# Attention kernel: the row sums' PSUM bank becomes a fourth work bank, and ScalarE copies the sums to SBUF

## The chip, the cores and the metric

The kernel runs on one core of one Trainium2 chip. The metric is the device time of one execution in microseconds. The kernel before took 1515.11 us, the median of three runs (1514.18 to 1516.34).

## What is computed

Two attention layers over a batch of 8 images of 256 channels and 1024 positions, in fp32. Layer 0 has a group normalisation and 8 heads of 32 channels; layer 1 has one head whose queries and keys have 32 channels and whose values have 256. Cut to what matters:

```python
# layer 0, B = 8, C = 256, T = 1024, 8 heads of ch = 32
h = groupnorm(x, 32 groups) * gn_w + gn_b
q, k, v = qkv_w @ h + qkv_b
w = softmax((q * ch**-0.25)^T (k * ch**-0.25))      # T x T for each head
x = x + proj_w @ (v w^T) + proj_b
# layer 1
energy = (Wq x)^T (Wk x)                             # T x T
x = x + gamma * (Wv x) softmax(energy)^T
```

## The kernel before

**Tiling.** An image's layer 0 is worked in two groups of four heads (g) and two chunks of 512 queries (c): four chunks, ci = 2g + c. A chunk goes over 8 blocks of 128 keys; for a block and a pair of heads there is one slot, in which TensorE makes two score products of 128 keys by 512 queries into PSUM (`st`, three banks used in turn), ScalarE takes the exponential of each into `probs` (a ring of nine slots in SBUF, line 789), and GpSimd adds the slots up into `acc` (lines 901 to 906 and 925). Every eight slots TensorE multiplies the exponentials with the values into the bank `pv` (line 574), in a group of 32 instructions. Layer 1 of the image before has eight slots of its own, 48 to 55, with products at line 596. So an image has 72 slots, and each slot has three stops.

**Maxima.** The softmax subtracts each query's maximum. It is found ahead of time: TensorE makes the same scores with queries on the partitions (lines 651 and 659), and VectorE reduces each bank (lines 954 and 957). That is 128 products per image in layer 0 and 16 in layer 1. The maxima are transposed (lines 664 and 667), split in two parts (lines 970 and 972) and put under the queries as two more rows by DMA.

**Work banks.** The maxima, their transposes, queries and keys (QK, line 714), values (VT, line 721; VT1, line 685), the projection (P, line 673) and the small products of the normalisation use a cycle of three PSUM banks, `work`. `fill_bank` (line 631) takes the next bank in turn, and TensorE waits there until the bank's last user, three entries before, has been read (`wait_used`). VectorE or ScalarE reads it; QK is read by both. ScalarE's own uses are counted apart (`SCALAR_USES`, line 156).

**Sums and quotients.** When a chunk's exponentials are added up in `acc`, a product with ones (`fill_rec`, line 605) sums them over the partitions into a bank of its own, `rec` (line 243). VectorE makes the reciprocals in place in PSUM in four pieces of 128 columns (line 1042; two pieces in layer 1, line 1054). After the last piece it multiplies `attn`, which ScalarE has copied from `pv`, with `rec` (line 1047). In layer 1 it multiplies each half of the raw output by gamma and `rec`, into `rec` (line 1060, twice), and adds `y` into `xa` (line 1063). Before a new sum TensorE waits for the last quotient (`wait_rec_free`, line 312). So these steps have one input in PSUM and one in SBUF. In the normalisation, lines 998 and 999 compute the same difference into PSUM and into SBUF, and line 1001 multiplies the two.

**Order.** Every engine has its own stream, in order. TensorE, ScalarE and VectorE go through the same plan (`plan_of`, line 106): tables by kind of image (`FIRST`, `STEADY`, `LAST`, `EPILOGUE`, lines 45 to 97) give for each entry of a chain the stop at which it stands, with 216 stops in an image. In the chain of sums an entry SUM is followed by its four reciprocals, in that of layer 1 by two. TensorE makes the sums of a slot at its end (line 735). ScalarE serves its entries behind the slot's exponentials, ahead of them in some slots (line 849). SP's queue issues the DMAs that stack queries and keys (24 for each group, `stack_rows`, line 390) and the transfers of inputs, maxima and output; GpSimd issues none.

```python
ST_BANKS, WORK_BANKS = 3, 3                                            # line 32
if i >= WORK_BANKS:                                                    # line 634
    wait_used(pe, banks[kind][i - WORK_BANKS], kind, b)
for e in ready:                                                        # line 735
    fill_rec(e, kind, b)
```

Of the kernel before, what the change touches and what calls it, by code (L numbers as in the profile page):

```python
# [5 lines left out]
F32 = mybir.dt.float32  # L6
# [25 lines left out]
ST_BANKS, WORK_BANKS = 3, 3  # L32
# [7 lines left out]
def places(*counts):  # L40
# [5 lines left out]
    "maxima1": (56, 60, 71, 73, 74, 76, 82, 99, 100, 101, 103, 103, 107, 108, 113, 114, 122, 125),  # L46
    "qk1": (193, 196, 196, 203),
    "norm": (27, 34, 35, 42, 52, 70, 84, 100, 109, 110, 120),
# [3 lines left out]
    "layer1": (4, 7, 32, 33, 38, 55, 88, 112, 139),  # L52
    "v1": (14, 16),
    "maxima": places(1, 0, 1, 2, 2, 2, 1, 0, 0, 1, 2, 2, 0, 0, 0, 3, 1, 1, 1, 1, 0, 0, 1, 0, 2, 0, 1, 0, 0, 0, 1,
# [6 lines left out]
}  # L61
FIRST = {
    "qf": (7, 7, 8, 8),
    "maxima0": (12, 12, 16, 21, 22, 22, 24, 24, 24, 24, 24, 26, 26, 28, 28, 28),
    "qk1": (158, 193, 208, 208),
    "norm": (29, 29, 29, 42, 48, 64, 64, 107, 108, 110, 112),
    "sums": (63, 72, 95, 97, 108, 112, 122, 151, 155, 157, 162, 166, 185, 203, 206),
    "v0": (193, 211),
    "v1": (32, 50),
    "maxima": places(4, 1, 0, 1, 1, 0, 0, 0, 0, 0, 0, 0, 0, 0, 0, 4, 0, 1, 0, 0, 0, 1, 0, 0, 2, 0, 0, 1, 0, 0, 1,  # L70
# [6 lines left out]
}  # L77
LAST = {
    "maxima1": (58, 60, 62, 63, 66, 73, 81, 82, 83, 88, 91, 94, 95, 95, 110, 112, 125, 125),
    "sums": (9, 11, 26, 30, 32, 56, 57, 67, 111, 122, 143, 152, 155, 155, 156, 163, 165, 166, 167, 167),  # L80
    "sums1": (159, 160, 163, 169, 170, 170, 171, 174, 174, 174, 175, 175),
    "layer1": (14, 24, 38, 39, 41, 67, 70, 106, 113),
    "v1": (32, 119),
    "maxima": places(0, 0, 2, 0, 2, 0, 0, 1, 0, 0, 3, 1, 1, 0, 1, 0, 0, 1, 0, 1, 2, 0, 2, 0, 0, 0, 0, 0, 3, 0, 1,
# [6 lines left out]
}  # L91
EPILOGUE = {
    "sums": (3, 3, 6, 6, 10),
# [12 lines left out]
def plan_of(kind):  # L106
# [1035 lines left out]
```

## Time and profile before

| | us |
|---|---|
| median of three runs | 1515.11 |
| lowest, highest run | 1514.18, 1516.34 |
| span of the profiled execution | 1513.1 |
| TensorE busy (matmuls) | 1476.9 |
| TensorE weight loads | 892.7 |
| GpSimd busy | 1168.3 |
| VectorE busy | 1099.3 |
| ScalarE busy | 745.2 |

The profiled execution's span goes from its first to its last instruction; no time of its own with what lies around it is given, so it is set beside the runs. Matmuls are pipelined and each is drawn longer than the distance to the next, so a busy TensorE is not one at its peak; how often weight loads wait, and for whom, says more. The other engines' busy times add up as they are. Line numbers such as L954 are those of the kernel. PE is TensorE, PEld its weight loads, DVE VectorE, ACT ScalarE, POOL GpSimd.

### The profile page before, as it was taken

What the parts mean: (1) busy time and instruction counts of PE and PEld (TensorE: products, weight loads), DVE (VectorE), ACT (ScalarE), POOL (GpSimd) and SP (SyncE); (2) the same over time, 40 slices, a digit from 0 to 9 for tenths busy, and PEclk for the clock granted to TensorE, in tenths of its full rate; (3) what the DMA queues carried; (4) which work ended last, traced back from release to release, by engine and by line L of the source; (5) the groups of instructions that cost most, each with busy time, mean ns of one, the idle gap of its engine ahead of it and who ended that gap; (6) DMA issues with size and microseconds to landing.
All of it is one profiled execution on the core that took longest, in us unless ns stands there. A gap on an engine that the chain in (4) does not pass through costs nothing.

```text
span 1513.1 us, 20608 instructions
## 1 busy us (share of the span) xinstructions
PE 1476.9 (98%) x7248; PEld 892.7 (59%) x7248; DVE 1099.3 (73%) x1922; ACT 745.2 (49%) x1373; POOL 1168.3 (77%) x540
## 2 busy tenths in 40 slices
PE   8899999999999999999999999999999999999988
PEld 6454455567555765558555675557655585556547
DVE  4777868787787878877687777878778776775343
ACT  2356446644566355653556445563546536554412
POOL 2278579985899678994899858997789949898704
PEclk8799999999999999999999999999999999999979
DMA  5223132120503014030421205030140303100100
GB/s 150 48 67 78 36 74 60 38 48 31 139 22 85 15 48 113 17 85 22 106 64 30 56 22 147 23 84 15 44 112 22 85 21 98 44 1 8 49 21 29
DMA packets 47143, 85.24 MB, mean 56 GB/s; under 512 B 11072, under 2 KB 21184, under 8 KB 47040
## 3 DMA queue, kind: packets, MB, share of 16 engines
q1 hardware_dynamic: 46896, 83.74, 22.0%
q8 instruction: 57, 0.93, 0.3%
q14 instruction: 46, 0.38, 0.1%
q10 hardware_dynamic: 144, 0.20, 0.1%
HBM read 18.29 MB, written 8.39 MB: 18 GB/s over the span
## 4 chain that ended last, share of the span: by engine, by line
PE 82%; DVE 8%; ACT 4%; SPq 2%; issue 2%; DMA 1%; POOL 0%; ACTq 0%; DVEq 0%; POOLq 0%
PE pv L596 15%; PE pv L574 15%; PE st L565 14%; PE work L651 13%; PE work L714 7%; DVE mpart L954 6%; PE work L673 3%; PE work L721 3%; PE work L685 3%; ACT probs L789 2%; PE st L557 2%; SPq L396 2%; PE rec L615 2%; PE work L659 2%; PE work L679 1%
## 5 line engine op out<-in xcount | busy, mean ns | idle before, releaser
L925 POOL TENSOR_TENSOR acc<-acc,probs 128x1024 f32<-128x1024 f32 x372 | 871.0, 2380 | 19.8 <-ACT probs L789 18.9
L789 ACT ACTIVATE probs<-st 128x512 f32<-128x512 f32 x1152 | 610.6, 602 | 422.1 <-PE st L565 201.2
L954 DVE TENSOR_REDUCE mpart<-work 128x1 f32<-128x512 f32 x1008 | 636.1, 678 | 136.3 <-PE work L651 133.8
L651 PE MATMUL work<-ks,qs 96*128 96x512 f32 x1008 | 430.5, 469 | 9.2 <-DMA ks<-part_hi 2.4
L565 PE MATMUL st<-qs,ks 98*128 98x512 f32 x1024 | 395.7, 429 | 7.0 <-DMA qs<-mrow 3.1
L925 POOL TENSOR_TENSOR acc<-probs 128x1024 f32<-128x1024 f32 x64 | 151.1, 2373 | 191.4 <-ACT probs L789 191.3
L651 PEld LDWEIGHTS work<-ks,qs 96*128 96x128 f32 x1008 | 190.6, 193 | 143.2 <-DVE mpart L954 68.0
L565 PEld LDWEIGHTS st<-qs,ks 98*128 98x128 f32 x1024 | 193.3, 191 | 119.1 <-ACT probs L789 65.3
L596 PE MATMUL pv<-probs,l_vt 128*128 128x256 f32 x1024 | 240.8, 381 | 0.7 <-ACT xa L862 0.5
L574 PE MATMUL pv<-probs,vt 128*32 128x512 f32 x2048 | 236.3, 602 | 0.0
L596 PEld LDWEIGHTS pv<-probs,l_vt 128*128 128x128 f32 x1024 | 193.8, 191 | 35.8 <-ACT probs L789 5.9
L901 POOL TENSOR_TENSOR acc<-probs 128x1024 f32<-128x1024 f32 x32 | 75.4, 2356 | 116.6 <-ACT probs L789 108.3
L574 PEld LDWEIGHTS pv<-probs,vt 128*32 128x32 f32 x2048 | 60.6, 111 | 139.6 <-issue 137.9
L1042 DVE RECIPROCAL rec<-rec 128x128 f32<-128x128 f32 x128 | 117.4, 941 | 7.4 <-PE rec L615 4.1
L714 PE MATMUL work<-h,wqkv 128*128 128x512 f32 x256 | 119.3, 600 | 2.0 <-ACT h L842 1.9
L984 DVE SCALAR_TENSOR_TENSOR part_lo<-work,qkbs,part_hi 128x512 fp32r<-128x512 f32 x60 | 44.4, 749 | 76.9 <-ACT part_hi L813 76.9
L957 DVE TENSOR_REDUCE mpart_l<-work 128x1 f32<-128x512 f32 x128 | 83.1, 679 | 20.7 <-PE work L659 20.4
L1054 DVE RECIPROCAL rec<-rec 128x128 f32<-128x128 f32 x64 | 57.5, 936 | 45.7 <-PE rec L628 45.7
L714 PEld LDWEIGHTS work<-h,wqkv 128*128 128x128 f32 x256 | 47.3, 191 | 47.7 <-issue 39.0
L813 ACT ACTIVATE part_hi<-work,qkbs 128x512 fp32r<-128x512 f32 x60 | 41.2, 687 | 65.3 <-PE work L714 65.3
L862 ACT COPY xa<-pv 128x512 f32<-128x512 f32 x32 | 18.8, 587 | 108.1 <-PE pv L596 108.1
L721 PEld LDWEIGHTS work<-wqkv,h 128*128 128x128 f32 x512 | 61.5, 192 | 4.1 <-ACT vt L818 1.4
(82 smaller groups left out, 953.4 us busy)
## 6 DMA issues: line engine op xcount, KB each, us to landing
qs<-part_hi SPq DMA_DIRECT2D x120, 128.0 KB, 2.4
ks<-part_hi SPq DMA_DIRECT2D x120, 128.0 KB, 2.4
xa<-in_x SPq DMA_DIRECT2D x16, 512.0 KB, 4.4
y<-in_x SPq DMA_DIRECT2D x8, 1024.0 KB, 6.1
out<-xa SPq DMA_DIRECT2D x32, 256.0 KB, 2.2
qs<-part_lo SPq DMA_DIRECT2D x60, 128.0 KB, 2.4
ks<-part_lo SPq DMA_DIRECT2D x60, 128.0 KB, 2.4
l_qs<-part_hi SPq DMA_DIRECT2D x32, 64.0 KB, 2.0
```

Source lines behind the costliest of these rows:

```text
L565: mm(bank, ks[g][0:ROWS, j, blk * P:(blk + 1) * P], qs[g][0:ROWS, c, j, :], start=True, stop=True).then_inc(s_st0, 1)
L574: last = mm(pv[CH * j:CH * (j + 1), :], vt[:, blk, g * P + CH * j:g * P + CH * (j + 1)], probs[:, (n - 1 + j // 2) % PRING, (j % 2) * HALF ...
L596: last = mm(pv[:, m * QUARTER:(m + 1) * QUARTER], vt1[:, 4 * (i % 2) + q, m * P:(m + 1) * P], probs[:, n % PRING, q * QUARTER:(q + 1) * QU ...
L651: last = mm(bank, qs[g][0:HI_HI_LO, c, j, tb * P:(tb + 1) * P], ks[g][0:HI_HI_LO, j, half * HALF:(half + 1) * HALF], start=True, stop=True)
L714: last = mm(bank, wqkv[:, k, col:col + P], h[:, k, n * HALF:(n + 1) * HALF], start=(k == 0), stop=(k == KT - 1))
L721: last = mm(bank[:, s * P:(s + 1) * P], h[:, k, blk * P:(blk + 1) * P], wqkv[:, k, 2 * C + g * P:2 * C + (g + 1) * P], start=(k == 0), sto ...
L789: nc.scalar.activation(probs[:, n % PRING, half * HALF:(half + 1) * HALF], st[:, (2 * n + half) % ST_BANKS, :], ACT.Exp).then_inc(s_exp1 i ...
L901: pool.tensor_tensor(a, probs[:, (n - 1) % PRING, :], probs[:, n % PRING, :], ALU.add).then_inc(s_add1, 1)
L925: pool.tensor_tensor(a, first, probs[:, n % PRING, :], ALU.add).then_inc(s_add0, 1)
L954: last = dve.reduce_max(mpart[:, 4 * j + tb, half:half + 1], bank, AX.X)
L957: last = dve.reduce_max(mpart1[:, tb, half:half + 1], bank, AX.X)
L1042: dve.reciprocal(r, r).then_inc(s_rec, 1)
```

## The change

The bank `rec` in PSUM is gone; `work` has four banks, and `rec` is a tensor of 512 columns in SBUF. The sums SUM and SUM1 are entries of the cycle of work banks now: `sum_rows` makes the same products into the next work bank, at the entry's own stop instead of the end of its slot. ScalarE copies the bank to `rec` (512 columns, or 256 in layer 1), and before it waits that the last quotient has been made; TensorE doesn't wait for that any more. VectorE's reciprocals and quotient steps are the same instructions, with `rec` in SBUF. VectorE waits for ScalarE's copy, GpSimd and the exponentials of the last part for the fill of the bank, instead of for the sums' own counter. At one point of the first image VectorE waits for its own reduction of the last early maximum (M0). The tables of stops are new throughout; the lines of sums in the steady images, and those of the second group's queries and keys (QF) in the first, are shown.

```diff
-ST_BANKS, WORK_BANKS = 3, 3
+ST_BANKS, WORK_BANKS = 3, 4
 STEADY = {
-    "sums": (10, 14, 14, 16, 23, 72, 74, 75, 100, 118, 134, 135, 135, 141, 146, 153, 154, 154, 154, 157),
-    "sums1": (159, 159, 159, 162, 164, 164, 170, 171, 175, 175, 193, 193),
+    "sums": (10, 14, 14, 16, 23, 72, 74, 75, 100, 119, 134, 135, 137, 141, 147, 154, 159, 159, 159, 159),
+    "sums1": (159, 162, 162, 162, 166, 166, 168, 168, 168, 171, 189, 193),
...
 FIRST = {
-    "qf": (7, 7, 8, 8),
+    "qf": (3, 3, 3, 5),
...
-NO_BANK = ("SUM", "SUM1", "MC", "MC1", "BN", "AGG", "H", "R", "R1")
-SCALAR_USES = ("VT", "VT1")
+NO_BANK = ("MC", "MC1", "BN", "AGG", "H", "R", "R1")
+SCALAR_USES = ("VT", "VT1", "SUM", "SUM1")
...
+        rec = sb("rec", [P, HALF])
...
-        rec = ctx.enter_context(nc.psum_tensor("rec", [P, HALF], F32))
...
-            eng.wait_ge(s_sum, sum_no(e, kind, b) + 1)
+            eng.wait_ge(s_w, w_base(kind, b) + place[kind][e] + 1)
...
-            def fill_rec(e, kind, b):
-
-                wait_rec_free(pe, e, kind, b)
-                if e[0] == "SUM":
...
+            def sum_rows(e, bank, kind, b):
+
+                if e[0] == "SUM1":
+                    pe.wait_ge(s_add1, ADDS1 * (b - 1) + 3 * (e[1] + 1))
+                    return mm(bank[:, 0:QUARTER], ones[:, :], acc1[e[1] % 2][:, 0:QUARTER], start=True, stop=True)
+                _, g, c = e
...
+                pe.wait_ge(s_add0, adds_until(bb, ci + 1) - (2 * LEFT if kind == "epilogue" else 0))
+                for j in range(GH):
+                    last = mm(bank[CH * j:CH * (j + 1), :], ones[:, 0:CH],
+                              acc[:, c, j // 2, (j % 2) * HALF:(j % 2 + 1) * HALF], start=True,
+                              stop=not left, tile_position=(0, CH * j))
...
+                elif what in ("SUM", "SUM1"):
+                    last = sum_rows(e, bank, kind, b)
...
-                    for e in ready:
-                        fill_rec(e, kind, b)
...
+                elif e[0] in ("SUM", "SUM1"):
+                    wait_rec_free(act, e, kind, b)
                 act.wait_ge(s_w, w_base(kind, b) + i + 1)
...
+                elif e[0] == "SUM":
+                    last = nc.scalar.copy(rec[:, :], bank)
+                elif e[0] == "SUM1":
+                    last = nc.scalar.copy(rec[:, 0:QUARTER], bank[:, 0:QUARTER])
...
                     if p == 0:
-                        wait_summed(dve, ("SUM", g, c), kind, b)
+                        wait_used(dve, ("SUM", g, c), kind, b)
...
                     if p == 0:
-                        wait_summed(dve, ("SUM1", c), kind, b)
+                        wait_used(dve, ("SUM1", c), kind, b)
...
+                    if kind == "first" and (g, c) == (0, 1):
+                        wait_used(dve, ("M0", 1, 3, 1), kind, b)
                     wait_used(dve, ("M", g, c, GH - 1, 3, 1), kind, b)
```

## Rows read from the trace of the kernel before

**Rows 1.** the head of the page: span, busy time of each engine

```profile
span 1513.1 us, 20608 instructions
...
PE 1476.9 (98%) x7248; PEld 892.7 (59%) x7248; DVE 1099.3 (73%) x1922; ACT 745.2 (49%) x1373; POOL 1168.3 (77%) x540
```

**Rows 2.** table by windows: the first image and a later one (us from the start)

```profile
core 0: us, PE busy (x) PEld busy (x) DVE busy (x) ACT busy (x) POOL busy (x), PEclk, DMA share, GB/s
58.00:240.00 182.00, 176.84 (x823) 87.28 (x823) 136.22 (x242) 92.97 (x171) 129.13 (x56) 0.97 0.29 71
417.00:594.00 177.00, 175.53 (x891) 108.40 (x890) 137.44 (x241) 92.71 (x171) 148.73 (x69) 1.00 0.24 59
```

**Rows 3.** timeline of TensorE: start us, us, instruction

```profile
487.51 0.39 PE L565 MATMUL st<-qs,ks 98*128 98x512 f32 x1
487.74 0.39 PE L651 MATMUL work<-ks,qs 96*128 96x512 f32 x1
```

**Rows 4.** table of waits, whole run: us in total, times, longest us

```profile
PEld work L651 <- DVE mpart L954: 68.0, 207, 0.8
PEld st L565 <- ACT probs L789: 65.3, 230, 0.8
...
PEld work L659 <- DVE mpart L954: 12.6, 20, 0.8
...
PEld work L651 <- DVE mpart_l L957: 9.2, 31, 0.6
```

**Rows 5.** table of waits, first image alone (58 to 240 us)

```profile
PEld work L651 <- DVE mpart L954: 21.7, 57, 0.8
```

**Rows 6.** groups of instructions: busy us, mean ns of one, idle before

```profile
L954 DVE TENSOR_REDUCE mpart<-work 128x1 f32<-128x512 f32 x1008 | 636.1, 678 | 136.3 <-PE work L651 133.8 <-issue 0.2
L789 ACT ACTIVATE probs<-st 128x512 f32<-128x512 f32 x1152 | 610.6, 602 | 422.1 <-PE st L565 201.2 <-PE pv L574 96.6 <-PE st L557 96.6
...
L651 PEld LDWEIGHTS work<-ks,qs 96*128 96x128 f32 x1008 | 190.6, 193 | 143.2 <-DVE mpart L954 68.0 <-issue 31.4 <-DVE mpart_l L957 9.2
...
L1042 DVE RECIPROCAL rec<-rec 128x128 f32<-128x128 f32 x128 | 117.4, 941 | 7.4 <-PE rec L615 4.1 <-PE rec L622 3.2
...
L1047 DVE TENSOR_TENSOR attn<-attn,rec 128x512 f32<-128x512 f32 x32 | 22.0, 687 | 1.8 <-ACT attn L872 0.7
L1070 DVE BATCH_NORM_STATS2 bst<-xa 128x6 f32<-128x512 f32 x32 | 20.2, 679 | 9.1 <-DMA xa<-in_x 9.1
...
L872 ACT COPY attn<-pv 128x512 f32<-128x512 f32 x32 | 18.8, 587 | 60.3 <-PE pv L574 60.3
```

**Rows 7.** timeline of GpSimd, 417 to 594 us

```profile
472.56 28.06 POOL L925 TENSOR_TENSOR acc<-acc,probs 128x1024 f32<-128x1024 f32 x12
...
515.35 2.35 POOL L901 TENSOR_TENSOR acc<-probs 128x1024 f32<-128x1024 f32 x1 [5.72 <-ACT probs L789]
517.77 1.28 POOL L904 TENSOR_TENSOR acc<-acc 128x512 f32<-128x512 f32 x1
519.14 0.73 POOL L906 TENSOR_TENSOR acc<-acc 128x256 f32<-128x256 f32 x1
...
543.94 28.02 POOL L925 TENSOR_TENSOR acc<-acc,probs 128x1024 f32<-128x1024 f32 x12
```

**Rows 8.** timeline of VectorE, same stretch: quotient steps

```profile
476.84 0.69 DVE L1047 TENSOR_TENSOR attn<-attn,rec 128x512 f32<-128x512 f32 x1
...
516.59 1.01 DVE L1060 SCALAR_TENSOR_TENSOR rec<-xa,gam,rec 128x256 f32<-128x256 f32 x2
...
551.27 1.01 DVE L1060 SCALAR_TENSOR_TENSOR rec<-xa,gam,rec 128x256 f32<-128x256 f32 x2
```

**Rows 9.** the chain in order of time: start us, us, what

```profile
514.74 3.45 PE pv L596 x16
519.57 3.45 PE pv L596 x16
...
551.82 3.57 PE pv L574 x32
```

More of the change, by code:

```diff
@@ L45 @@
 STEADY = {
-    "maxima1": (56, 60, 71, 73, 74, 76, 82, 99, 100, 101, 103, 103, 107, 108, 113, 114, 122, 125),
-    "qk1": (193, 196, 196, 203),
-    "norm": (27, 34, 35, 42, 52, 70, 84, 100, 109, 110, 120),
-    "sums": (10, 14, 14, 16, 23, 72, 74, 75, 100, 118, 134, 135, 135, 141, 146, 153, 154, 154, 154, 157),
-    "sums1": (159, 159, 159, 162, 164, 164, 170, 171, 175, 175, 193, 193),
-    "v0": (181, 206),
-    "layer1": (4, 7, 32, 33, 38, 55, 88, 112, 139),
-    "v1": (14, 16),
-    "maxima": places(1, 0, 1, 2, 2, 2, 1, 0, 0, 1, 2, 2, 0, 0, 0, 3, 1, 1, 1, 1, 0, 0, 1, 0, 2, 0, 1, 0, 0, 0, 1,
[6 rows of a table removed]
+    "maxima1": (56, 60, 69, 74, 74, 76, 82, 96, 104, 104, 104, 104, 107, 108, 113, 114, 116, 123),
@@ L61 @@
+    "qk1": (189, 192, 195, 203),
+    "norm": (25, 26, 27, 42, 52, 69, 84, 98, 106, 110, 120),
+    "sums": (10, 14, 14, 16, 23, 72, 74, 75, 100, 119, 134, 135, 137, 141, 147, 154, 159, 159, 159, 159),
+    "sums1": (159, 162, 162, 162, 166, 166, 168, 168, 168, 171, 189, 193),
+    "v0": (181, 206),
+    "layer1": (4, 7, 29, 33, 38, 55, 89, 112, 138),
+    "v1": (12, 16),
+    "maxima": places(2, 0, 0, 2, 2, 3, 1, 0, 0, 2, 2, 0, 0, 0, 0, 3, 1, 1, 1, 1, 0, 0, 0, 1, 2, 0, 1, 0, 0, 0, 0, 2, 1,
[6 rows of a table added]
 }
@@ L62 @@
 FIRST = {
-    "qf": (7, 7, 8, 8),
[L64 to L70, printed above, removed]
[6 rows of a table removed]
+    "qf": (3, 3, 3, 5),
+    "maxima0": (8, 8, 8, 8, 8, 10, 14, 14, 14, 15, 22, 23, 25, 26, 27, 27),
@@ L77 @@
+    "qk1": (159, 190, 205, 210),
+    "norm": (29, 29, 29, 42, 48, 59, 62, 105, 105, 107, 109),
+    "sums": (67, 72, 96, 98, 103, 113, 123, 149, 156, 158, 163, 164, 186, 205, 208),
+    "v0": (190, 212),
+    "v1": (31, 48),
+    "maxima": places(4, 1, 0, 1, 1, 0, 0, 0, 0, 0, 0, 2, 0, 0, 0, 2, 0, 1, 0, 0, 0, 1, 0, 0, 0, 3, 0, 0, 1, 0, 0, 0, 0,
[6 rows of a table added]
 }
 LAST = {
-    "maxima1": (58, 60, 62, 63, 66, 73, 81, 82, 83, 88, 91, 94, 95, 95, 110, 112, 125, 125),
-    "sums": (9, 11, 26, 30, 32, 56, 57, 67, 111, 122, 143, 152, 155, 155, 156, 163, 165, 166, 167, 167),
@@ L81 @@
[L81 to L84, printed above, removed]
[6 rows of a table removed]
+    "maxima1": (58, 60, 62, 62, 62, 76, 77, 82, 83, 88, 93, 94, 95, 95, 109, 111, 121, 126),
+    "sums": (9, 11, 26, 30, 32, 56, 57, 67, 110, 121, 144, 145, 151, 154, 155, 162, 165, 165, 168, 169),
+    "sums1": (159, 160, 161, 169, 170, 170, 171, 174, 174, 174, 175, 178),
@@ L91 @@
+    "layer1": (4, 22, 34, 37, 43, 67, 71, 107, 113),
+    "v1": (12, 105),
+    "maxima": places(0, 0, 2, 0, 2, 0, 0, 1, 0, 0, 2, 0, 0, 0, 4, 1, 0, 1, 0, 2, 2, 0, 0, 0, 0, 0, 4, 0, 0, 0, 0, 0, 0,
[5 rows of a table added]
 }
 EPILOGUE = {
-    "sums": (3, 3, 6, 6, 10),
[3 rows of a table removed]
+    "sums": (2, 2, 2, 2, 2),
[3 rows of a table added]
 }
@@ L603, in product_l1 @@
                         fill_bank(e, kind, b)
-            def fill_rec(e, kind, b):
-                wait_rec_free(pe, e, kind, b)
-                if e[0] == "SUM":
-                    _, g, c = e
-                    ci = 2 * g + c
-                    bb = b - 1 if ci == 3 else b
-                    left = LEFT if kind == "epilogue" else 1 if bb == 0 else 0
-                    pe.wait_ge(s_add0, adds_until(bb, ci + 1) - (2 * LEFT if kind == "epilogue" else 0))
-                    for j in range(GH):
-                        last = mm(rec[CH * j:CH * (j + 1), :], ones[:, 0:CH],
-                                  acc[:, c, j // 2, (j % 2) * HALF:(j % 2 + 1) * HALF], start=True,
-                                  stop=not left, tile_position=(0, CH * j))
-                    if left:
-                        wait_exp(pe, last_slot(ci), bb)
-                    for blk in range(left):
-                        for j in range(GH):
-                            last = mm(rec[CH * j:CH * (j + 1), :], ones[:, 0:CH],
-                                      probs[:, (last_slot(ci) - 2 * left + 1 + 2 * blk + j // 2) % PRING,
-                                            (j % 2) * HALF:(j % 2 + 1) * HALF],
-                                      start=False, stop=blk == left - 1, tile_position=(0, CH * j))
-                else:
-                    pe.wait_ge(s_add1, ADDS1 * (b - 1) + 3 * (e[1] + 1))
-                    last = mm(rec[:, 0:QUARTER], ones[:, :], acc1[e[1] % 2][:, 0:QUARTER], start=True, stop=True)
-                last.then_inc(s_sum, 1)
@@ new lines, in sum_rows @@
+            def sum_rows(e, bank, kind, b):
[3 more added lines that the diff above has]
+                _, g, c = e
+                ci = 2 * g + c
+                bb = b - 1 if ci == 3 else b
+                left = LEFT if kind == "epilogue" else 1 if bb == 0 else 0
+                pe.wait_ge(s_add0, adds_until(bb, ci + 1) - (2 * LEFT if kind == "epilogue" else 0))
[3 more added lines that the diff above has]
+                              stop=not left, tile_position=(0, CH * j))
+                if left:
+                    wait_exp(pe, last_slot(ci), bb)
+                for blk in range(left):
+                    for j in range(GH):
+                        last = mm(bank[CH * j:CH * (j + 1), :], ones[:, 0:CH],
+                                  probs[:, (last_slot(ci) - 2 * left + 1 + 2 * blk + j // 2) % PRING,
+                                        (j % 2) * HALF:(j % 2 + 1) * HALF],
+                                  start=False, stop=blk == left - 1, tile_position=(0, CH * j))
+                return last
@@ L728, in step @@
                     stops = [[e for e in plans[kind][STOPS * n + k] if e[0] not in NO_BANK] for k in range(STOPS)]
-                    ready = [e for k in range(STOPS) for e in plans[kind][STOPS * n + k] if e[0] in ("SUM", "SUM1")]
                     for half in range(2):
@@ L915, in step @@
                         if ci == 0 and kind != "first":
-                            pool.wait_ge(s_sum, sum_no(sums[kind][0], kind, b))
+                            wait_summed(pool, ("SUM", 1, 0), "first" if b == 1 else "steady", b - 1)
                         elif ci == 1 and kind != "first":
@@ L1090, in step @@
                     for e in entries:
-                        if e[0] in ("H", "SUM", "SUM1"):
+                        if e[0] == "H":
                             continue
```

1 line of the change is left out of this document (removed), and 41 rows, old and new, of tables (EPILOGUE, FIRST, LAST, STEADY).

## The prediction

> **What bounds the kernel now.** I read the page's head first. TensorE is busy for all but 36 us of 1513.1, VectorE for 73% [rows 1]. A busy TensorE is not one at its peak, so next come two stretches of the table by windows: the first image, 182 us, and a later one, 177 us; here all engines but TensorE have room on average, GpSimd least (148.7 of 177) [rows 2]. How fast TensorE can go is seen where nothing is late, in its timeline: score and maxima products of 512 columns start some 0.23 us apart (487.51, 487.74), though each is drawn 0.39 us long [rows 3]. What holds it beyond that is in the table of waits, in the rows of the weight loads: 68.0 us in 207 waits for VectorE's maxima over work banks, 12.6 and 9.2 us more of the same sort, and 65.3 us in 230 waits for ScalarE's exponentials over score banks [rows 4]. A load has about 0.05 us between it and the next anyway (0.24 less the 0.19 that it takes [rows 6]), so these waits are stalls less 0.05 us each. Work banks: 89.8 us in 258 waits, less 13, is 77 us, some 5% of the time. That is the ceiling for a fourth work bank. Of it, 21.7 us in 57 waits, 19 after the same deduction, lie in the first image [rows 5]; some 58 us are spread over the rest.
>
> **The change, part by part.** The sum is made against the profiled span of 1513.1 us; the runs shown lie 1.1 to 3.2 us above it, their median 2.0.
>
> *A fourth work bank, tables anew.* A maximum holds its bank for VectorE's 678 ns [rows 6], while TensorE makes a product in 0.24. Every further bank lets a burst run on for one more reduction, which takes 0.68 − 0.24 = 0.44 us off the waits of that burst. Outside the first image the waits average 0.33 us and come in twos and threes, so one bank should remove most: I take two thirds of 58, 38 us. In the first image bursts are long, and there VectorE's rate decides: 8 of 19. Gain 46 us. Bounds: none (the stalls turn into other waits) and 77. The new tables move entries by a few stops, with what they issue: the second group's queries and keys of the first image go from stops 7 to 8 to stops 3 to 5, and the 24 stacking transfers on SP's queue behind them start earlier; nothing is queued there that is due before. I cost this at nothing beyond the bank's gain.
>
> *64 sums in the cycle of banks.* The same products, with the same changes of tile, so no TensorE time. TensorE no longer waits for the quotient before a sum, but for a work bank. It waited little for quotients before, so nothing is won.
>
> *64 copies on ScalarE.* 32 of 512 columns at 587 ns [rows 6], 18.8 us; 32 of 256 columns, between 0.29 (half) and 0.587 us, I take 0.37, 11.8 us. ScalarE is busy 92.7 of 177 us [rows 2], so most of these 31 us are covered by its idle time. But a copy can stand in front of an exponential for which TensorE waits. It waits for 230 of 1152 [rows 4, 6], a fifth, and not each of those has a copy before it: I take a tenth, 3 us; bounds 0 and 31.
>
> *The wait for the last quotient moves to ScalarE.* Exponentials are queued behind it, and TensorE, GpSimd and the score banks wait for these. The sum of group 1, chunk 0 has its four reciprocals all at stop 159, beside the first layer-1 sum, whose copy waits for that quotient: four times 0.94 us and 0.69 us [rows 6] is 4.5 us of VectorE in front of it. Three score banks and the lag of two slots between scores and products give TensorE about one layer-1 slot, 4.8 us (product groups start 514.74 and 519.57 on the chain [rows 9]), so I take 0; the bound above is 2 us in each of 7 images, 14.
>
> *192 reciprocals in SBUF.* In PSUM 128 columns take 941 ns. 512 columns out of SBUF (batch statistics, 679 ns) and out of PSUM (maxima, 678 ns) cost VectorE the same [rows 6]; I take 0, between the 0.1 us each (19 us of VectorE time) that I could not exclude either way. The Trainium skill, page "VectorE: DVE Perf Modes", section on the TRN2 errata, gives a fixed 58 cycles for sources in SBUF and 120 for PSUM; by it the reciprocals would win 65 ns each, 12 us of VectorE time in all, which the two equal rows speak against.
>
> *128 quotient steps with two inputs in SBUF.* These are the 32 of line 1047, 64 of line 1060, 32 of line 1063. Until now each has one input in PSUM, and so has every other large VectorE operation here with two tensors; lines 998 and 999 even make the same difference twice, into PSUM and into SBUF, so that the product of the two has one of each. What a second SBUF input costs beside GpSimd, which reads SBUF all the time, no row shows. Lower bound 0: VectorE takes 0.49 or 0.69 us as now. Upper bound: each waits for the end of GpSimd's addition in progress, and GpSimd's next one slips in between two of them. Laid over one image: additions run back to back from 472.56, 2.34 us each; a chain 515.35 to 517.70, then 1.28, then 0.73; again without a break from 543.94 [rows 7]. Of an image's eight quotients three find GpSimd idle. Of the layer-1 ones, that at 516.59 would wait 1.1 + 1.3 + 0.7 = 3.1 us, that at 551.27 2.0 + 2.3 + 2.3 = 6.6; three of layer 0, as at 476.84 with its 0.4 [rows 8], 0.9 together. That is 10.6 us in an image, 74 in seven. At 516.59 the products of layer 1 fill 3.45 of the 4.8 us of a slot [rows 9] and leave work banks free. That at 551.27 meets a full stretch, but 3.57 us of it lie under the product group from 551.82, which needs no work bank [rows 9]. So 6.6 − 3.6 = 3.0 us reach TensorE in each image. I take this upper case for VectorE: 21 us over seven images. Bounds 0 and 74.
>
> *The small rest.* Line 1083 of VectorE waits once for a reduction of its own queue, long done. Waits on the fill counters replace those on the sums' counter at the same moments. GpSimd would be held for the quotient steps themselves, 1.7 us at the last one of an image, ahead of its own idle time. All at nothing; cover: GpSimd's 28 us of idle time in an image [rows 2].
>
> Sum: −46 + 3 + 0 + 0 + 21 = −22. 1513.1 − 22 = 1491, with 2 around the span **1493 us**.
>
> **Rivals.**
> *Slower: the quotient steps wait, and what is queued behind them waits too.* Place: the end of each quotient, from line 1047 on. Price: the whole 10.6 us an image, 74 us, if the stretches around them are dense, plus 14 for ScalarE's stand behind the quotient, less 46 won: +42, some 1557; with half of the 74, plus 14 and 3, it is +8, 1523. It decides from the point where more than 46 − 3 = 43 us of waits reach TensorE, 6 us an image. For it: VectorE goes from 137.4 to 148 of 177 us, and reciprocals, reductions and quotients share one queue; the last steps hold query and key banks, too. Against it: half of the layer-1 quotients meet no addition, and the rest lie beside products. The Trainium skill states the mechanism ("SBUF — State Buffer", section "SBUF: two separate sides"): VectorE with two SBUF inputs and a GpSimd operation that reads SBUF exclude each other for a whole instruction. By that rule the quotient waits worked out above are real, and only their reach is open. Middle of this case: 1535. Chance 0.32.
> *Faster than forecast: the second SBUF input costs nothing.* Then −46 + 3 = −43, or 1472; with the ceiling of the bank 1450 at most. For it: no row shows any contention. Chance 0.17.
> *No change: the stalls move.* Waits for score banks are nearly as many (65.3 us in 230 [rows 4]), and a TensorE that is held less by work banks may only reach those sooner; or gain and price cancel. 1512 to 1518. Chance 0.12.
> *Forecast.* The bank's gain is seen, the quotients cost some of it: 1480 to 1510. Chance 0.39.
>
> **Numbers.** Likeliest 1493. Below, the range takes in the case without contention (1470); above, it goes into the slower case to 1540. About 0.2% is what a measurement of this kernel can tell from no change. Faster 0.39 + 0.17 = 0.56; same 0.12; slower 0.32.
>
> **What would show it.** Weight loads' waits for work banks should fall from 90 to some 45 us. The quotient steps should start late after their reciprocals, or be drawn longer than 0.49 and 0.69 us, where GpSimd is in an addition, and GpSimd's additions beside them longer than 2.4 us: were all still 0.49 and 0.69 without gaps, the contention is refuted. ScalarE should be busy some 31 us more. Waits for exponentials much over 65 us, with ScalarE waiting for the quotient, would show its queue as the new bound. If VectorE's waits stay and the time still rises, the forecast is wrong by the reach of the quotient steps.

## The result and the profile after

The changed kernel takes 1674.97 us (median of four runs, 1672.45 to 1681.12), against 1514.71 us for the kernel before on the same chip: a ratio of 1.1067, 95% interval [1.1042, 1.1092]. It was forecast at 1493 us, in a range from 1470 to 1540. The profiled execution spans 1670.6 us, 157.5 more than before. Every ratio in this document is that of fast runs alone; a run more than 1.5% above the fastest one of its kernel counts as slow, and two runs below do.

The head of the page of the kernel after, and TensorE's granted clock in 40 slices:

```profile
span 1670.6 us, 20737 instructions
...
PE 1501.0 (90%) x7248; PEld 928.4 (56%) x7248; DVE 1296.0 (78%) x1922; ACT 772.5 (46%) x1437; POOL 1175.6 (70%) x540
...
PEclk8799989898998989989899899989999899899989
```

Beside [rows 1], TensorE is idle for 169.6 us instead of 36.2, and VectorE is busy 196.7 us more. The mean granted clock of the profiled execution went from 0.978 to 0.932. With the two levels of 2.4 and 1.2 GHz (1 and 0.5) that is 0.044 and 0.136 of the span at the lower one, an estimate of 67 and 227 us.

The groups of instructions of the kernel after (busy us, mean ns of one | idle before); the lines are some numbers further down than in [rows 6]:

```profile
L926 POOL TENSOR_TENSOR acc<-acc,probs 128x1024 f32<-128x1024 f32 x372 | 871.6, 2378 | 119.2 <-ACT probs L784 118.8
L955 DVE TENSOR_REDUCE mpart<-work 128x1 f32<-128x512 f32 x1008 | 632.2, 678 | 126.6 <-PE work L647 125.0
...
L1048 DVE TENSOR_TENSOR attn<-attn,rec 128x512 f32<-128x512 f32 x32 | 157.3, 4916 | 1.1
...
L1043 DVE RECIPROCAL rec<-rec 128x128 f32<-128x128 f32 x128 | 115.1, 926 | 20.5 <-ACT rec L827 20.5
L1061 DVE SCALAR_TENSOR_TENSOR rec<-xa,gam,rec 128x256 f32<-128x256 f32 x64 | 93.7, 1465 | 5.7 <-ACT xa L863 3.5
...
L1064 DVE TENSOR_TENSOR xa<-rec,y 128x512 f32<-128x512 f32 x32 | 27.0, 845 | 1.1
...
L827 ACT COPY rec<-work 128x512 f32<-128x512 f32 x32 | 18.7, 585 | 18.5 <-PE work L614 10.2 <-PE work L621 7.2 <-DVE xa L1064 0.2
...
L829 ACT COPY rec<-work 128x256 f32<-128x256 f32 x32 | 11.9, 373 | 38.2 <-PE work L607 23.3 <-DVE xa L1064 9.9 <-PE work L647 4.1
```

Everything but the quotient steps has its old duration, the reciprocals out of SBUF too (926 ns after 941). The 32 products of line 1048 took 4916 ns each, after 687 [rows 6]; those of line 1061 took 1465 after 490, those of 1064 took 845 after 691. In sum VectorE stood in these three lines for 135.3 + 62.4 + 4.9 = 203 us longer. How the 203 us are spread matters: 23 of the 128 steps were drawn over 3.2 us long, 17 of line 1048 and 6 of line 1061, and they hold 182 us of it. GpSimd's additions still take 2.38 us on average: it hardly waited for VectorE. ScalarE's copies cost 18.7 + 11.9 us, as forecast.

The table of waits of the kernel after (us in total, times, longest us):

```profile
ACT probs L784 <- PE st L563: 346.1, 171, 26.4
...
PEld work L647 <- DVE part_lo L985: 93.7, 14, 8.3
...
PE work L647 <- DVE part_lo L985: 87.2, 13, 7.9
...
PEld work L647 <- DVE mpart L955: 55.4, 132, 1.5
```

Waits of the weight loads for maxima fell from 68.0 us in 207 times [rows 4] to 55.4 in 132. That is no clean measure of the fourth bank, since TensorE stood still elsewhere; the run with one-input steps below gives one. In their place stand fourteen waits, up to 8.3 us long, for a bank of queries or keys (part_lo), whose reader on VectorE, in the place shown next, is queued behind a quotient step; the two rows for them tell of the same waits, once at the weight load and once at the product. ScalarE, for its part, waits 346 us for scores, after 201.2 [rows 6].

One such place, first on GpSimd's timeline of the kernel after (start us, us, instruction):

```profile
504.11 16.26 POOL L926 TENSOR_TENSOR acc<-acc,probs 128x1024 f32<-128x1024 f32 x7
```

on VectorE's:

```profile
507.26 0.94 DVE L1043 RECIPROCAL rec<-rec 128x128 f32<-128x128 f32 x1
508.23 12.69 DVE L1048 TENSOR_TENSOR attn<-attn,rec 128x512 f32<-128x512 f32 x1
520.85 0.74 DVE L985 SCALAR_TENSOR_TENSOR part_lo<-work,qkbs,part_hi 128x512 fp32r<-128x512 f32 x1
```

on ScalarE's:

```profile
523.58 0.60 ACT L784 ACTIVATE probs<-st 128x512 f32<-128x512 f32 x1 [8.77 <-PE st L563]
```

on TensorE's:

```profile
513.10 0.73 PE L563 MATMUL st<-qs,ks 98*128 98x512 f32 x2
521.64 1.39 PE L647 MATMUL work<-ks,qs 96*128 96x512 f32 x2 [7.80 <-DVE part_lo L985]
...
524.97 0.63 PE L647 MATMUL work<-ks,qs 96*128 96x512 f32 x1
525.39 0.63 PE L563 MATMUL st<-qs,ks 98*128 98x512 f32 x1
...
528.43 0.39 PE L647 MATMUL work<-ks,qs 96*128 96x512 f32 x1
528.66 0.40 PE L563 MATMUL st<-qs,ks 98*128 98x512 f32 x1
```

and in the table by windows over the same stretch:

```profile
core 0: us, PE busy (x) PEld busy (x) DVE busy (x) ACT busy (x) POOL busy (x), PEclk, DMA share, GB/s
...
516.00:520.00 4.00, 0.00 (x0) 0.00 (x0) 4.00 (x1) 0.00 (x0) 4.00 (x2) 0.71 0.00 0
520.00:524.00 4.00, 2.36 (x5) 1.72 (x6) 3.97 (x8) 0.42 (x1) 0.38 (x1) 0.50 0.29 66
524.00:528.00 4.00, 4.00 (x14) 1.40 (x14) 2.32 (x4) 1.88 (x4) 2.55 (x2) 0.51 0.61 135
528.00:532.00 4.00, 4.00 (x18) 3.19 (x18) 3.29 (x5) 2.77 (x6) 4.00 (x2) 1.00 0.88 197
```

The product of line 1048 starts at 508.23 and ends at 520.92. All that time GpSimd goes through seven additions without a gap (504.11 to 520.37), and 0.55 us after the last the product is done. So it didn't wait only for the addition in progress, which ended at 508.8; it waited for that one and the five behind it. The reader of the keys' bank follows at 520.85, and TensorE, which had come to that bank at 513.8, starts again at 521.64. GpSimd's run ended because of that: TensorE's standstill stopped the scores, and ScalarE had waited 8.77 us for them when it made its next exponential at 523.58. The granted clock falls while TensorE stands (0.71 in the window from 516, no product in it) and is 0.50 and 0.51 in the windows to 528, its lower level: two products of 512 columns are 0.42 us apart there (524.97, 525.39), and 0.23 us again at 528.43 and 528.66, at the upper one. Of the 128 quotient steps 17 were drawn over 8 us long, and with all 17 the granted clock falls to 0.50, during the step or within 0.2 us of its end.

**Not every addition goes first.** Another step of line 1048, on GpSimd's timeline and on VectorE's:

```profile
841.63 2.39 POOL L926 TENSOR_TENSOR acc<-acc,probs 128x1024 f32<-128x1024 f32 x1 [0.33 <-ACT probs L784]
843.99 2.82 POOL L926 TENSOR_TENSOR acc<-acc,probs 128x1024 f32<-128x1024 f32 x1
```

```profile
843.00 1.57 DVE L1048 TENSOR_TENSOR attn<-attn,rec 128x512 f32<-128x512 f32 x1
```

These two additions follow each other without idle time, too. Yet the product got in between them: it was done 0.55 us after the first, and the second was drawn 2.82 us instead of 2.38. The timelines of the whole run have 77 ends of an addition at which a quotient step was waiting and the next addition followed without idle time. At 69 of them the addition went first, at 8 the step. Count the additions of an unbroken run from the one that starts after idle time, be it 0.08 us. Then all 69 are ends of the third or a later addition of an unbroken run; four of the 8 are ends of a first and two of a second, and the other two are a third and a fourth right behind steps that had been let in. The runs below say the same: no end of a first or second addition was passed over in any, and none of a fifth or later one let a step in. So it takes an unbroken run of some length, three to five additions here, before VectorE is starved. Why that is so no run shows.

### The profile page after: what moved, and what is told of

It reads as the page before. It is cut to its first block, busy times and chain, and to the rows that moved or that the text cites. A ratio compares the mean times of both kernels' runs of the same rounds, so it can differ in the third digit from the quotient of the medians.

```text
span 1670.6 us, 20737 instructions
## 1 busy us (share of the span) xinstructions
PE 1501.0 (90%) x7248; PEld 928.4 (56%) x7248; DVE 1296.0 (78%) x1922; ACT 772.5 (46%) x1437; POOL 1175.6 (70%) x540
## 4 chain that ended last, share of the span: by engine, by line
PE 67%; DVE 19%; issue 7%; SPq 4%; ACT 2%; DMA 1%; ACTq 0%; DVEq 0%; POOL 0%; POOLq 0%
PE pv L594 13%; PE st L563 12%; PE work L647 11%; PE pv L572 8%; DVE mpart L955 6%; PE work L712 6%; DVE rec L1061 4%; PE work L669 4%; DVE attn L1048 3%; PE work L681 3%; SPq L394 2%; PE work L614 2%; DVE rec L1043 2%; PE work L719 2%; PE work L655 2%
## 5 line engine op out<-in xcount | busy, mean ns | idle before, releaser
L926 POOL TENSOR_TENSOR acc<-acc,probs 128x1024 f32<-128x1024 f32 x372 | 871.6, 2378 | 119.2 <-ACT probs L784 118.8
L647 PE MATMUL work<-ks,qs 96*128 96x512 f32 x1008 | 421.4, 470 | 97.5 <-DVE part_lo L985 87.2
L563 PE MATMUL st<-qs,ks 98*128 98x512 f32 x1024 | 416.1, 451 | 6.2 <-DMA qs<-mrow 3.1
L647 PEld LDWEIGHTS work<-ks,qs 96*128 96x128 f32 x1008 | 198.0, 200 | 220.9 <-DVE part_lo L985 93.7
L563 PEld LDWEIGHTS st<-qs,ks 98*128 98x128 f32 x1024 | 199.5, 198 | 139.2 <-ACT probs L784 63.9
L1048 DVE TENSOR_TENSOR attn<-attn,rec 128x512 f32<-128x512 f32 x32 | 157.3, 4916 | 1.1
L712 PE MATMUL work<-h,wqkv 128*128 128x512 f32 x256 | 131.4, 642 | 2.0 <-ACT h L843 1.9
L1061 DVE SCALAR_TENSOR_TENSOR rec<-xa,gam,rec 128x256 f32<-128x256 f32 x64 | 93.7, 1465 | 5.7 <-ACT xa L863 3.5
L669 PE MATMUL work<-attn,wproj 128*128 128x512 f32 x128 | 69.6, 674 | 24.5 <-DVE mpart L955 17.3
L712 PEld LDWEIGHTS work<-h,wqkv 128*128 128x128 f32 x256 | 52.7, 207 | 46.7 <-issue 39.1
```

The costliest lines, as they stand in the source:

```text
L563: mm(bank, ks[g][0:ROWS, j, blk * P:(blk + 1) * P], qs[g][0:ROWS, c, j, :], start=True, stop=True).then_inc(s_st0, 1)
L647: last = mm(bank, qs[g][0:HI_HI_LO, c, j, tb * P:(tb + 1) * P], ks[g][0:HI_HI_LO, j, half * HALF:(half + 1) * HALF], start=True, stop=True)
L669: last = mm(bank, wproj[:, k, m * P:(m + 1) * P], attn[:, k, n * HALF:(n + 1) * HALF], start=(k == 0), stop=(k == KT - 1))
L712: last = mm(bank, wqkv[:, k, col:col + P], h[:, k, n * HALF:(n + 1) * HALF], start=(k == 0), stop=(k == KT - 1))
L926: pool.tensor_tensor(a, first, probs[:, n % PRING, :], ALU.add).then_inc(s_add0, 1)
L1048: dve.tensor_tensor(a, a, rec[:, :], ALU.mult).then_inc(s_quot, 1)
```

## The experiments

Two theories. **A:** a VectorE step with two SBUF inputs waits until GpSimd has no addition running or ready; an unbroken run starves it, and that is the whole loss. (The place at 843.00 shows that A is too strong in its first half; the experiments ask about the second.) **B:** the loss comes from the other parts: ScalarE's copies and its waits for the last quotient, or the new tables. The time before in the groups of runs was 1512.37 to 1513.19 us.

| kernel | us | ratio to before, 95% interval |
|---|---|---|
| before, reciprocals in SBUF | 1711.17 | 1.1314 [1.1297, 1.1331] |
| before, layer 0's reciprocals in SBUF | 1645.05 | 1.0874 [1.0857, 1.0891] |
| before, reciprocals in SBUF, gaps on GpSimd | 1576.43 | 1.0419 [1.0396, 1.0442] |
| before, one-input steps | 1512.61 | 0.9996 [0.9986, 1.0007] |
| changed, one-input steps | 1492.2 | 0.9864 [0.9843, 0.9885] |
| changed, gaps on GpSimd | 1570.9 | 1.0398 [1.0355, 1.0441] |
| changed, gaps near quotients (lower two of four runs) | 1559.15 | 1.0303 [1.0265, 1.0341] |
| changed, three work banks | 1704.06 | 1.1259 [1.1237, 1.1281] |
| changed, three work banks, sums in PSUM | 1604.07 | 1.0608 [1.0592, 1.0624] |
| changed, two score banks, sums in PSUM | 1602.22 | 1.0593 [1.0573, 1.0613] |
| changed, layer 0's quotients on GpSimd | 1605.26 | 1.0611 [1.0579, 1.0643] |
| the same, and layer 1's last | 1588.4 | 1.0489 [1.0472, 1.0507] |

**Only the second SBUF input, in the kernel before.** Tables, banks and TensorE's part stay.

```diff
+        recs = sb("recs", [P, HALF])
...
-                    dve.reciprocal(r, r).then_inc(s_rec, 1)
+                    dve.reciprocal(recs[:, p * PIECE:(p + 1) * PIECE], rec[:, p * PIECE:(p + 1) * PIECE]).then_inc(s_rec, 1)
...
-                        dve.tensor_tensor(a, a, rec[:, :], ALU.mult).then_inc(s_quot, 1)
+                        dve.tensor_tensor(a, a, recs[:, :], ALU.mult).then_inc(s_quot, 1)
```

The same for lines 1054, 1060 and 1063.

> The kernel before, with its three work banks, tables and PSUM bank for the sums; only the reciprocals are written to SBUF, so that the 128 quotient steps have two SBUF inputs. Theory A (a quotient step waits until GpSimd's unbroken run of additions ends, up to 12 us): the whole loss and more is here, 1640 to 1720 us, with steps of line 1047 of several us on average. Theory B (the loss comes from ScalarE's copies, its waits for the last quotient, and the new tables): within 0.5% of before, 1510 to 1522 us. My recorded upper case (each waits for one addition only): 1530 to 1550 us.

Measured 1711.17 us: the whole loss and more, as A says, with only this one tensor moved to SBUF. Its groups of quotient steps:

```profile
L1047 DVE TENSOR_TENSOR attn<-attn,recs 128x512 f32<-128x512 f32 x32 | 129.6, 4051 | 1.8 <-ACT attn L873 0.7
...
L1059 DVE SCALAR_TENSOR_TENSOR recs<-xa,gam,recs 128x256 f32<-128x256 f32 x64 | 86.9, 1357 | 4.6 <-ACT xa L863 2.4
...
L1062 DVE TENSOR_TENSOR xa<-recs,y 128x512 f32<-128x512 f32 x32 | 27.4, 857 | 1.1
```

107.6 + 55.6 + 5.3 = 168.5 us of VectorE beyond [rows 6] cost 199 us of time. B is out as the main cause: none of its parts is in this kernel.

**The same for layer 0 alone**, which leaves lines 1054 to 1063 as they were.

```diff
-                    dve.reciprocal(r, r).then_inc(s_rec, 1)
+                    dve.reciprocal(recs[:, p * PIECE:(p + 1) * PIECE], rec[:, p * PIECE:(p + 1) * PIECE]).then_inc(s_rec, 1)
```

> The kernel before with only the reciprocals of layer 0 in SBUF, so that 32 of the 128 steps (line 1047) have two SBUF inputs. In the run with all 128 these 32 took 108 us of the 169 us of VectorE time gained, and the time rose by 199 us. If the time goes with VectorE's delay: 1620 to 1660 us. If the layer-1 steps, behind which query and key banks wait, are what hurts: below 1600 us.

Measured 1645.05 us. Its groups:

```profile
L1047 DVE TENSOR_TENSOR attn<-attn,recs 128x512 f32<-128x512 f32 x32 | 129.9, 4058 | 1.8 <-ACT attn L873 0.7
...
L1060 DVE SCALAR_TENSOR_TENSOR rec<-xa,gam,rec 128x256 f32<-128x256 f32 x64 | 31.3, 489 | 4.6 <-ACT xa L863 2.4
```

The 32 steps took 107.9 us more and cost 132.5 us of time, 1.23 us for each us; the layer-1 steps, one input in PSUM again, are back at 489 ns. The other 66 us of the run with all 128 go with the 61 us of the layer-1 steps, 1.09 for each. The expectation by VectorE's delay holds (1620 to 1660); both layers cost somewhat more than the delay itself.

**The changed kernel with steps of one SBUF input.** Each quotient step is a maximum over its SBUF operand; the division by the sums, gamma and the last addition are left out.

```diff
-                        dve.tensor_tensor(a, a, rec[:, :], ALU.mult).then_inc(s_quot, 1)
+                        dve.reduce_max(one[:, :], a, AX.X).then_inc(s_quot, 1)
```

> The changed kernel with each of the 128 quotient steps replaced by a maximum over the SBUF operand alone (512 columns for lines 1048 and 1064, 256 for 1061); the division by the sums, gamma and the last addition are left out. Theory A: the steps take 0.69 and 0.41 us, the time falls to 1465 to 1500 us, below before. Theory B: 1640 to 1680 us.

Measured 1492.2 us, as A says. Its groups, and a row of its waits:

```profile
L1044 DVE RECIPROCAL rec<-rec 128x128 f32<-128x128 f32 x128 | 115.1, 926 | 11.8 <-ACT rec L828 11.8
...
L1062 DVE TENSOR_REDUCE one<-xa 128x1 f32<-128x256 f32 x64 | 26.9, 420 | 5.6 <-ACT xa L864 3.5
...
L1049 DVE TENSOR_REDUCE one<-attn 128x1 f32<-128x512 f32 x32 | 22.0, 686 | 1.1
```

```profile
PEld work L648 <- DVE mpart L956: 53.2, 116, 0.8
```

Reciprocals from SBUF to SBUF and maxima out of SBUF don't wait beside GpSimd (926 and 686 ns). The waits over work banks that the prediction counted, 89.8 us in 258 times [rows 4], are 54.6 us in 121 times here, 53.2 of them in the row shown. The same replacement in the kernel before is the control:

```diff
-                        dve.tensor_tensor(a, a, rec[:, :], ALU.mult).then_inc(s_quot, 1)
+                        dve.reduce_max(one[:, :], a, AX.X).then_inc(s_quot, 1)
```

> Control for the changed kernel with one-input steps: the kernel before with the same 128 quotient steps replaced by maxima over the SBUF operand alone (division, gamma and the last addition left out). If the replacement itself is neutral: 1508 to 1514 us, and the 1492 us of its counterpart are the net gain of the fourth bank, the copies and the new tables. If the replaced steps themselves save time: near 1500 us or below, and that gain is smaller.

Measured 1512.61 us, the time before, so the replacement itself is neutral. Bank, copies and tables together win 20.4 us, and the second SBUF input costs 1675 − 1492 = 183 us on top.

**Gaps in GpSimd's stream.** Each layer-0 addition waits for the completion of the one before on its own engine.

```diff
+                    if issued[0]:
+                        pool.wait_ge(s_add0, issued[0])
+                    issued[0] += 1
                     pool.tensor_tensor(a, first, probs[:, n % PRING, :], ALU.add).then_inc(s_add0, 1)
```

> The changed kernel, with one wait more in front of each layer-0 addition on GpSimd: for the completion of its own previous addition, so that additions no longer stand back to back. Theory A: a VectorE step gets in at the next gap, after 2.4 us at most; steps of line 1048 average 1.5 to 2.5 us instead of 4.9, and the time falls to 1500 to 1570 us. Theory B: 1675 us or more, since GpSimd only gets slower. If what counts is GpSimd's busy share and not its gaps: 1660 to 1690 us.

Measured 1570.9 us, at the upper edge of what A expects and over 100 us faster than the changed kernel, though nothing was done but to make GpSimd wait. GpSimd's timeline, VectorE's, and the groups of this run (its profiled execution was the slowest of the four, 1582.81 us):

```profile
483.35 2.38 POOL L931 TENSOR_TENSOR acc<-acc,probs 128x1024 f32<-128x1024 f32 x1 [0.17 <-POOL acc L931]
485.90 2.61 POOL L931 TENSOR_TENSOR acc<-acc,probs 128x1024 f32<-128x1024 f32 x1 [0.17 <-POOL acc L931]
```

```profile
483.37 2.91 DVE L1053 TENSOR_TENSOR attn<-attn,rec 128x512 f32<-128x512 f32 x1
```

```profile
L1066 DVE SCALAR_TENSOR_TENSOR rec<-xa,gam,rec 128x256 f32<-128x256 f32 x64 | 55.3, 865 | 5.7 <-ACT xa L863 3.5
...
L1053 DVE TENSOR_TENSOR attn<-attn,rec 128x512 f32<-128x512 f32 x32 | 48.0, 1499 | 1.1
...
L1069 DVE TENSOR_TENSOR xa<-rec,y 128x512 f32<-128x512 f32 x32 | 39.5, 1234 | 1.1
```

Additions are 2.55 us apart, 0.17 us of it idle. The product at 483.37 waits for the one addition in progress (to 485.73) and is done 0.55 us later, at 486.28, while the next addition is drawn 0.23 us longer: it was held. In the whole run no step was passed over; the longest was drawn 2.91 us. The steps took 26.0 + 24.0 + 17.4 = 67 us more than in [rows 6], a third of the 203 us, and near the 74 us that the prediction had as its bound. The time lies 79 us above the 1492 without two-input steps. GpSimd's slower stream has a part in it: TensorE waits 26.5 us, in 6 times, for its additions before a sum. How much of the 79 is these waits, the 67 us and a lower clock (0.953, after 0.977 with one-input steps) was not taken apart. In the kernel before with its reciprocals in SBUF, the same wait:

```diff
+                    if issued[0]:
+                        pool.wait_ge(s_add0, issued[0])
```

> The kernel before with all reciprocals in SBUF (1711 us) and GpSimd's extra wait for its own previous addition before each layer-0 addition. Starvation by unbroken runs: the steps wait for one addition at most, as in my recorded bound, and the time falls to 1550 to 1610 us. If the runs' gaps don't matter in this layout: 1700 us or more.

Measured 1576.43 us, after 1711.17, as expected of starvation by unbroken runs. Two of its groups show steps that wait about once instead of starving:

```profile
L1064 DVE SCALAR_TENSOR_TENSOR recs<-xa,gam,recs 128x256 f32<-128x256 f32 x64 | 61.6, 963 | 4.6 <-ACT xa L863 2.4
...
L1052 DVE TENSOR_TENSOR attn<-attn,recs 128x512 f32<-128x512 f32 x32 | 49.7, 1553 | 1.8 <-ACT attn L873 0.7
```

**Gaps only in the slots from a quotient's last reciprocal on.**

```diff
+                near = {n + d for n in last for d in range(4)}
...
+                    if issued[0] and n in near:
+                        pool.wait_ge(s_add0, issued[0])
```

> The changed kernel with the extra wait of GpSimd for its own previous addition only in the slot of a quotient's last reciprocal and the three behind it. If the position of the gaps is all that counts: VectorE's steps as with gaps everywhere (1.5 us for line 1048), GpSimd idle less than the 52 us of that run, time 1545 to 1571 us. If gaps elsewhere were needed, because GpSimd lags by more than three slots: 1571 to 1640 us.

The four runs took 1554.47, 1563.83, 1581.77 and 1588.10 us. The two lower ones, whose ratio stands in the table, lie in the first expectation, the two upper ones in the second. The steps of line 1048 averaged 2171 ns in the profile (of the run of 1563.83 us), against 1499 with gaps everywhere: some quotients met unbroken additions still, which the first expectation ruled out. So gaps near the quotients do at least most of the work, and whether gaps elsewhere help or hurt is open.

**The number of work banks.** Three banks in the changed kernel:

```diff
-ST_BANKS, WORK_BANKS = 3, 4
+ST_BANKS, WORK_BANKS = 3, 3
```

> The changed kernel with three work banks instead of four, all else the same (sums in SBUF, new tables). If starved quotient steps and the missing bank add up, as 1675 plus the 112 us by which the three-bank kernel without contention (1604) lies above the four-bank one without contention (1492): 1740 to 1800 us. If a starved VectorE makes the number of banks indifferent: 1675 to 1700 us.

Measured 1704.06 us, 4 us above the second expectation and 36 below the first. And with three banks and the copied sums in a PSUM bank, so that no step has two SBUF inputs:

```diff
-ST_BANKS, WORK_BANKS = 3, 4
+ST_BANKS, WORK_BANKS = 3, 3
...
-        rec = sb("rec", [P, HALF])
+        rec = ctx.enter_context(nc.psum_tensor("rec", [P, HALF], F32))
```

> The changed kernel with its tables, its sums in a work bank and ScalarE's 64 copies and waits, but the copies go to a PSUM bank of their own and work has three banks: no quotient step has two SBUF inputs. Theory A: 1505 to 1545 us. Theory B: 1640 to 1690 us, as the changed kernel.

Measured 1604.07 us: neither expectation. No quotient step waits (688 and 489 ns), so A's part holds. But tables laid out for four banks, and sums in the cycle, cost 92 us against before when there are three. Within these tables the fourth bank is worth 112 us without contention (1604 to 1492) and 29 with it (1704 to 1675): the delays don't add up. The starvation itself is less with three banks: the steps of line 1048 averaged 2153 ns there, not 4916. Why was not followed up. How much of the 92 us is the tables and how much the sums that take a work bank was not separated.

**A score bank given up instead.**

```diff
-ST_BANKS, WORK_BANKS = 3, 4
+ST_BANKS, WORK_BANKS = 2, 4
...
-        rec = sb("rec", [P, HALF])
+        rec = ctx.enter_context(nc.psum_tensor("rec", [P, HALF], F32))
```

> The changed kernel with four work banks and the copied sums in a PSUM bank of their own, paid with one of the three score banks (two left): no step has two SBUF inputs. If a work bank is worth more than a score bank, as 1604 against 1492 us for the fourth work bank in these tables suggests: 1500 to 1560 us. If the third score bank carries the overlap of TensorE and ScalarE: 1560 to 1700 us.

Measured 1602.22 us, in the second expectation. A row of its waits:

```profile
PEld st L563 <- ACT probs L784: 203.3, 475, 1.1
```

Waits for exponentials tripled (65.3 us in 230 times [rows 4]); in these tables the third score bank is worth as much as the fourth work bank, 110 us (1602 to 1492).

**Quotients on GpSimd.** No VectorE step of layer 0 has two SBUF inputs then; GpSimd makes the product in its stream, a slot behind the last reciprocal.

```diff
+            def quotient(e, kind, b):
+                _, g, c, _ = e
+                n = chunk_no(e, b)
+                pool.wait_ge(s_rec, PIECES * (n + 1))
+                pool.wait_ge(s_copy0, n + 1)
+                a = attn[:, g, c * HALF:(c + 1) * HALF]
+                pool.tensor_tensor(a, a, rec[:, :], ALU.mult).then_inc(s_quot, 1)
```

> The changed kernel, with the 32 quotient steps of layer 0 (line 1048) made by GpSimd in its own stream, one slot after the last reciprocal (for group 1, chunk 1 in the same slot), 1.28 us each as its other additions of 512 columns. Theory A (VectorE waits out GpSimd's unbroken runs): the 135 us that line 1048 took beyond its 0.69 us vanish, the 8.4 us per image at layer 1's last quotient stay: 1530 to 1590 us. If GpSimd's own load is what binds: above 1620 us.

Measured 1605.26 us, between the two expectations. And with layer 1's last quotient there, too:

```diff
+                for m in range(KT):
+                    pool.tensor_tensor(raw1(c)[:, m, :], raw1(c)[:, m, :], rec[:, 0:QUARTER],
+                                       ALU.mult).then_inc(s_sc1, 1)
+                pool.wait_ge(s_sc1, 2 * n + 2)
+                pool.tensor_tensor(raw1(c), raw1(c),
+                                   y[:, :, c * QUARTER:(c + 1) * QUARTER], ALU.add).then_inc(s_quot, 1)
```

> As the kernel with layer 0's quotients on GpSimd, and the last quotient of layer 1 there, too: ScalarE's copy of that sum is scaled by 1/gamma, and GpSimd makes two products of 256 columns and one addition of 512, 2.7 us per image. Theory A: no long VectorE wait is left; 1492 (quotients replaced by steps with one input) plus GpSimd's 8 us more per image where it is behind: 1490 to 1525 us. If GpSimd becomes the bound: 1530 to 1580 us.

Measured 1588.4 us, 63 above what theory A allowed and 8 above the range for a bound on GpSimd. Waits and GpSimd's timeline of this run:

```profile
ACT rec L835 <- POOL attn L902: 44.2, 8, 5.8
...
ACT rec L829 <- POOL attn L902: 25.7, 11, 4.3
...
PE work L671 <- POOL attn L902: 14.5, 9, 5.6
```

```profile
639.36 28.11 POOL L965 TENSOR_TENSOR acc<-acc,probs 128x1024 f32<-128x1024 f32 x12
667.43 4.70 POOL L965 TENSOR_TENSOR acc<-probs 128x1024 f32<-128x1024 f32 x2
672.09 11.73 POOL L965 TENSOR_TENSOR acc<-acc,probs 128x1024 f32<-128x1024 f32 x5
683.78 1.26 POOL L902 TENSOR_TENSOR attn<-attn,rec 128x512 f32<-128x512 f32 x1
685.01 16.38 POOL L965 TENSOR_TENSOR acc<-acc,probs 128x1024 f32<-128x1024 f32 x7
```

No starvation is left (no VectorE step with two SBUF inputs is drawn over 2.8 us), but from 639.36 to 701 GpSimd works without a pause, behind the exponentials. A quotient queued in it comes late (683.78), and ScalarE's next copy of a sum (44.2 and 25.7 us) and the projection (14.5 us) wait for it. The quotient's waiting moved to another queue; whether that is all of the 96 us above 1492 was not tested. A version that keeps the 20 us was not found: the PSUM operand of the quotient steps is what the eighth bank was for.

## Why the prediction was wrong, point by point

- **The step that failed** is the upper bound of the "128 quotient steps with two inputs in SBUF": "each waits for the end of GpSimd's addition in progress, and GpSimd's next one slips in between two of them". Behind an unbroken run of three to five additions or more, the step was passed over by one, three or five further additions, to the end of the run. The bound of 74 us of VectorE time was no bound: 203 us were measured, 182 of them in 23 such steps. With gaps in GpSimd's stream the bound was right, 67 us.
- **Where it failed.** For the steps of layer 0 the prediction had 0.9 us an image, some 6 in seven, and 135 were measured. For layer 1 it had 3.1 + 6.6 us an image, 68 in seven, and 67 were measured (62.4 + 4.9). That match is luck: in the kernel after, the last quotient of a later image is passed over by three additions in one go (a step drawn 8.91 us instead of 0.49) where three short waits were forecast, and the others wait less than forecast.
- **Reach.** The prediction let 3.0 of 10.6 us an image through to TensorE, on the ground that a product group covers the rest. Measured, nearly all of VectorE's delay or more became time: 183 us for 203 in the changed kernel, 199 for 168.5 and 132.5 for 107.9 in the kernel before. Cover that hides 2 us doesn't hide 12, and the long standstills are followed by products at 1.2 GHz, 0.42 us apart. In the changed kernel some 160 us more of the span lie at that level than before, part of them while TensorE stood; how much of the loss is the clock's alone was not measured apart. The prediction had no term for it.
- **The Trainium skill's rule** ("SBUF — State Buffer", section "SBUF: two separate sides"), that the two exclude each other for a whole instruction, agrees with the trace (the product at 483.37 is done only 0.55 us after the addition in progress, and the addition behind it is drawn 2.61 instead of 2.38 us). The section doesn't say who goes next when GpSimd has another instruction ready; at 508.23 GpSimd did, five times in a row, at 843.00 VectorE.
- **The slower rival** named the right place, the end of each quotient, and priced it at 1535, at most 1557. It was given 0.32 and should have had the larger part; its price failed with the same step. Its 14 us for ScalarE's stand behind the quotient are shown by no run. In the rival at 1472 the limit of 1450 "with the ceiling of the bank" is a slip: 1515 − 77 + 3 is 1441.
- **The fourth bank** was put at −46 with 3 for the copies, −43 in sum. Its net, with copies and tables, is −20.4 us (1512.6 to 1492.2 between the two kernels with one-input steps): the right sign, half the size. The waits that it counted fell from 89.8 us in 258 times to 54.6 in 121; less 0.05 us each, that is 77 and 49, so 28 us of stalls went and not 46. Why only 20 us of time came of it, where the copies were given 3, stays open.
- **The copies** cost 30.6 us of ScalarE as forecast (31), and the reciprocals didn't change (926 against 941 ns). The 65 ns each that the Trainium skill's page "VectorE: DVE Perf Modes", section on the TRN2 errata, would give them, an estimate from its fixed cycles for the two sources, were 15 in the trace.
- **The wait for the last quotient on ScalarE** was put at 0. It shows as 9.9 us of ScalarE waiting for line 1064 in the kernel after. No run prices it alone; the kernel with one-input steps has the wait and still gains.
- **The other rivals.** The contention is there, so the rival at 1472 is refuted. "The stalls move" is refuted, too: without the contention the time falls by 20 us, clear of the scatter of the runs.

## What to carry to other kernels

Where GpSimd runs back to back on SBUF operands, give every long VectorE operation at most one SBUF tensor: a PSUM bank that only serves as second operand can earn its place, as here (183 us against 20). Before a price is bounded by "the operation in progress", ask what the other engine has queued behind it, and how long it can go on without a pause. And price a standstill of TensorE that is longer than the gaps it had with what its clock takes afterwards.

## What the hardware showed that was not expected

- A VectorE product with two SBUF inputs was drawn up to 12.75 us instead of 0.69 (12.69 in the place shown), through five further GpSimd additions of 2.3 us each, and came in only when GpSimd had nothing ready. At the end of a first or second addition of an unbroken run it was never passed over.
- A pause of 0.17 us between additions let it in every time (the run with gaps has 40 such places); so did the 0.08 us between the additions of layer 1 (20 places in the kernel after).
- GpSimd loses little: its additions averaged 2378 ns in the changed kernel, 2380 before. An addition right behind a step that got in is longer (2.82 us in the place shown).
- VectorE's reciprocals from SBUF to SBUF (926 ns) and maxima out of SBUF (686 ns) are untouched by GpSimd's additions.
- The granted clock fell to 0.50 during a standstill of 7.8 us, and TensorE's first work after it, from 521.64 to 528, ran at that level.
